# The residual rows behind the first attention: no longer stored by the second projection stage, made again by the last stage

## The chip, the cores and the metric

The kernel is one program on one core of one Trainium2 chip (trn2). TensorE (PE in the profile) does the matmuls, VectorE is DVE, ScalarE is ACT, GpSimd is POOL, and SyncE (SP) only issues transfers. The metric is the device time of one execution in microseconds, lower is better. All data are float32.

## The reference, cut to what matters

Four sub-layers stand one behind the other; each ends with `x = x + layernorm(sublayer(layernorm(x)))` over 4 x 2048 rows of 256 features. The change touches the end of the third and the fourth:

```python
x = x + _layernorm(_L1_attn_ref(_layernorm(x), wq, wk, wv))     # third: attention with 16 heads
x = x + _layernorm(_L1_ffn_ref(_layernorm(x), ...))             # fourth: attention in 4 slices

# inside _L1_ffn_ref, of each slice e of 512 tokens, m = 256 / 2**e
out = einsum('bnm,om->bno', attn_out[:, sl, :m], o_w[:m, :m]) + o_b[:m]   # padded with zeros to 256
outs.append(out + x[:, sl, :])
```

With a = the first attention's output, and x2 the rows ahead of it, the rows behind it are x3 = x2 + a * rstd(a) - mean(a) * rstd(a), where rstd is one over the root of variance plus 1e-5, per row. They are needed twice: in the projections of the fourth sub-layer, and in its last step.

## The kernel before

Rows are worked on in 16 groups of 512 (four of the batch's slices e = 0 to 3, for each of four batch entries b). A group is a tile of 128 partitions by 4 rows (J) by 256 features, 512 KB. The program is a row of stages (`phase_...`), with a barrier of all engines between two of them; each has one in-order instruction list per engine, written out by hand, with semaphores between the lists. Nothing reorders them.

**phase_sliced** (L1354) runs behind the first attention. SP loads a group of `ao1` into A and of `x2` into X, three buffers each (L1415, L1418). DVE takes statistics of A; POOL makes rstd (RS0, L1467 and L1469); DVE adds, X = A * RS0 + X (L1586), and makes NB0 = -mean * RS0 (L1590). The rows in X still lack the shift NB0; the statistics and projections that follow don't need it, since a layernorm takes it out. ACT's `shifted` (L1543) adds it with four Identity instructions of 128x256 into XS (L1544), and SP's `store` (L1423) writes XS to `x3`. Beside it the group goes through a second layernorm (DVE L1596 to L1608), is turned by PE (L1506), copied by ACT (L1551), projected by PE (L1522, L1528), and split into high and low parts (ACT L1560, DVE L1618), which SP stores (L1434, L1438). ACT's list is, for each g: shifted, copy_turned, high. SP's: load(g + 2), store(g), store_qkv(g - 1).

**phase_attention** is the second attention and lies between the two stages that change.

**phase_final** (L2233) loads the attention's output (AT) and `x3` (X, four buffers, L2278), projects AT on PE (L2313), and for each group g: DVE's `add` biases the product (L2353) and makes Z = X * scale + product in the columns below m (L2359); ACT's `rest` makes Z in the other columns (L2326; nothing for e = 0); DVE's `stats` (L2368, L2372); POOL makes the reciprocal root RS with two small instructions (L2298, L2301); DVE's `result` makes NB (L2379) and Z = Z * RS + X (L2383, signals y_done); ACT adds NB into XO (L2339) and issues the store (L2342). The lists:

```python
# DVE:  add(0) stats(0); each g: add(g + 1), stats(g + 1), result(g)
# ACT:  rest(1);         each g: rest(g + 2), XO(g) once y_done(g), wait for XO(g), issue its store
# POOL:                  each g: VE(g), RS(g) once the statistics of g are there
# SP:   load_x(g + 1) waits for result(g - 3), then load_a(g + 1)
```

Of the kernel before, what the change touches and what calls it, by code (L numbers as in the profile page):

```python
# [5 lines left out]
F32 = mybir.dt.float32  # L6
F32R = mybir.dt.float32r
ALU = mybir.AluOpType
# [3 lines left out]
P = 128  # L12
B, T, D = 4, 2048, 256
TOK = B * T
# [1338 lines left out]

def phase_sliced(nc, ao_d, x_d, xnew_d, scales, ident_d, w_d, bias_d, nw_d, nb_d, qk_d, v_d):  # L1354

# [5 lines left out]
    with ExitStack() as ctx:  # L1361
        m = Mem(nc, ctx, tag)
        A = [m.sb(f"A{u}", [P, J, D]) for u in range(NX)]
        X = [m.sb(f"X{u}", [P, J, D]) for u in range(NX)]
        XS, XI = ([m.sb(f"{q}{u}", [P, J, D]) for u in range(2)] for q in ("XS", "XI"))
        XT = [m.sb(f"XT{u}", [P, CC, GT]) for u in range(2)]
        ST0, ST1 = (m.sb(q, [P, J, 6]) for q in ("ST0", "ST1"))
        MV0, MV1 = (m.sb(q, [P, J, 2]) for q in ("MV0", "MV1"))
        VE0, RS0 = (m.sb(q, [P, J]) for q in ("VE0", "RS0"))
        VE1 = m.sb("VE1", [P, 2, J])  # L1370
        NB0 = [m.sb(f"NB0{u}", [P, J]) for u in range(2)]
        nhalf = m.sb("nhalf", [P, 2, J])
# [15 lines left out]
            "const_ld", "half_set", "stat0", "stat1", "var0", "var1", "eps0", "eps1", "rs0", "rs1"))  # L1388
        nb0_done, x_sum, xs_done, xi_done, turned, xt, proj, vproj = (m.sem(n) for n in (
            "nb0_done", "x_sum", "xs_done", "xi_done", "turned", "xt", "proj", "vproj"))  # L1390
        hi_done, lo_done, v_done, nb_wide, w_scaled, b_put, b_done = (m.sem(n) for n in (
            "hi_done", "lo_done", "v_done", "nb_wide", "w_scaled", "b_put", "b_done"))
        a_ld, x_ld = ([m.sem(f"{n}{u}") for u in range(NX)] for n in ("a_ld", "x_ld"))
        xs_st, l_st = ([m.sem(f"{n}{u}") for u in range(2)] for n in ("xs_st", "l_st"))
        block = ctx.enter_context(nc.Block())
# [14 lines left out]
        def _(sp):  # L1410
            def load(g):
                b, e = divmod(g, E4)
                u = g % NX
                wait(sp, x_sum, g - NX + 1)
                sp.dma_start(A[u][:, :, :], ao_d[b][:, e * J:(e + 1) * J, :]).then_inc(a_ld[u], 16)  # L1415
                wait(sp, xi_done, g - NX + 1)
                wait(sp, xs_done, g - NX + 1)
                sp.dma_start(X[u][:, :, :], group(held(x_d), g)).then_inc(x_ld[u], 16)  # L1418

            def store(g):  # L1420
                u = g % 2
                wait(sp, xs_done, g + 1)
                sp.dma_start(group(held(xnew_d), g), XS[u][:, :, :]).then_inc(xs_st[u], 16)  # L1423

# [24 lines left out]
            for g in range(NGR):  # L1449
                if g + 2 < NGR:  # L1450
                    load(g + 2)
                store(g)
                if g > 0:
                    store_qkv(g - 1)
            store_qkv(NGR - 1)
            for u in range(2):
                sp.wait_ge(xs_st[u], 8 * NGR)
                sp.wait_ge(l_st[u], 40 * NGR)

        @block.gpsimd  # L1460
        def _(pool):
            nc.gpsimd.memset(nhalf[:, :, :], -0.5).then_inc(half_set, 1)
            pool.wait_ge(half_set, 1)

            def scale0(g):
                wait(pool, var0, g + 1)
                nc.gpsimd.tensor_scalar(VE0[:, :], MV0[:, :, 1], EPS, None, ALU.add).then_inc(eps0, 1)  # L1467
                wait(pool, eps0, g + 1)
                nc.gpsimd.tensor_tensor(RS0[:, :], VE0[:, :], nhalf[:, 0, :], ALU.pow).then_inc(rs0, 1)  # L1469

            def scale1(g):
                wait(pool, var1, g + 1)
                nc.gpsimd.tensor_scalar(VE1[:, 0, :], MV1[:, :, 1], 1.0 + EPS, EPS * EPS, ALU.mult,
                                        ALU.add).then_inc(eps1, 1)
                nc.gpsimd.tensor_scalar(VE1[:, 1, :], MV1[:, :, 1], EPS, None, ALU.add).then_inc(eps1, 1)
                wait(pool, eps1, 2 * g + 2)
                nc.gpsimd.tensor_tensor(scales[:, g, :, :], VE1[:, :, :], nhalf[:, :, :], ALU.pow).then_inc(rs1, 1)

            scale0(0)
            for g in range(NGR):  # L1480
                scale1(g)
                if g + 1 < NGR:
                    scale0(g + 1)
# [53 lines left out]
        def _(act):  # L1537
            def shifted(g):
                u = g % 2
                wait(act, x_sum, g + 1)  # L1540
                wait(act, nb0_done, g + 1)
                wait(act, xs_st[u], 16 * (g // 2))
                for j in range(J):  # L1543
                    ins = nc.scalar.activation(XS[u][:, j, :], X[g % NX][:, j, :], ACT.Identity,  # L1544
                                               bias=NB0[u][:, j:j + 1])
                ins.then_inc(xs_done, 1)

            def copy_turned(g):
# [15 lines left out]
            for g in range(NGR):  # L1564
                shifted(g)
                copy_turned(g)
                high(g)

        @block.vector
        def _(dve):  # L1570
# [10 lines left out]
            def add(g):  # L1581
                u = g % NX
                wait(dve, rs0, g + 1)
                wait(dve, x_ld[u], 16 * (g // NX + 1))
                for j in range(J):
                    ins = nc.vector.scalar_tensor_tensor(out=X[u][:, j, :], in0=A[u][:, j, :], scalar=RS0[:, j:j + 1],  # L1586
                                                         in1=X[u][:, j, :], op0=ALU.mult, op1=ALU.add)
                ins.then_inc(x_sum, 1)
                wait(dve, xs_done, g - 1)
                nc.vector.scalar_tensor_tensor(out=NB0[g % 2][:, :], in0=MV0[:, :, 0], scalar=-1.0, in1=RS0[:, :],  # L1590
                                               op0=ALU.mult, op1=ALU.mult).then_inc(nb0_done, 1)

# [639 lines left out]

def phase_final(nc, ao_d, ow_d, ob_d, scales, x_d, out_d):  # L2233

# [4 lines left out]
    with ExitStack() as ctx:  # L2239
        m = Mem(nc, ctx, tag)  # L2240
        AT = [m.sb(f"AT{u}", [P, CC, GT]) for u in range(3)]
        X = [m.sb(f"X{u}", [P, J, D]) for u in range(NX)]
        Z = [m.sb(f"Z{u}", [P, J, D]) for u in range(NZ)]
        XO = [m.sb(f"XO{u}", [P, J, D]) for u in range(2)]
# [10 lines left out]
                               "eps", "rs", "y_done", "nb_done", "xo_done"))  # L2255
        x_ld = [m.sem(f"x_ld{u}") for u in range(NX)]
        a_ld = [m.sem(f"a_ld{u}") for u in range(3)]
        o_st = [m.sem(f"o_st{u}") for u in range(2)]
# [7 lines left out]
        def _(sp):  # L2266
# [8 lines left out]

            def load_x(g):
                wait(sp, y_done, g - NX + 1)
                sp.dma_start(X[g % NX][:, :, :], group(held(x_d), g)).then_inc(x_ld[g % NX], 16)  # L2278
# [13 lines left out]
        @block.gpsimd  # L2292
        def _(pool):
            nc.gpsimd.memset(nhalf[:, :], -0.5).then_inc(half_set, 1)
            pool.wait_ge(half_set, 1)
            for g in range(NGR):
                wait(pool, var, g + 1)
                nc.gpsimd.tensor_scalar(VE[g % 2][:, :], MV[g % 2][:, :, 1], EPS, None, ALU.add).then_inc(eps, 1)  # L2298
                wait(pool, eps, g + 1)
                wait(pool, nb_done, g - 1)  # L2300
                nc.gpsimd.tensor_tensor(RS[g % 2][:, :], VE[g % 2][:, :], nhalf[:, :], ALU.pow).then_inc(rs, 1)  # L2301
# [16 lines left out]
        def _(act):  # L2318
            def rest(g):
                e, u = g % E4, g % 2  # L2320
                if e == 0:
                    return
                wait(act, x_ld[g % NX], 16 * (g // NX + 1))
                wait(act, xo_done, g - NZ + 1)
# [3 lines left out]
                ins.then_inc(rest_done, 1)  # L2328

            rest(1)  # L2330
            for g in range(NGR):
                u = g % 2
                if g + 2 < NGR:
                    rest(g + 2)
                wait(act, y_done, g + 1)
# [11 lines left out]
        def _(dve):  # L2347
            def add(g):
# [6 lines left out]
                wait(dve, biased, g + 1)  # L2355
                wait(dve, x_ld[g % NX], 16 * (g // NX + 1))
                wait(dve, xo_done, g - NZ + 1)
# [38 lines left out]
def sandwich(nc, d, out_d):  # L2396
# [4 lines left out]
    ycat = dram("ycat", [2 * CC, P, TOK])  # L2401
    x1, xn2, x2, x3 = (dram(n, [TOK, D]) for n in ("x1", "xn2", "x2", "x3"))
    logits, routed = (dram(n, [B, EXPERTS, T]) for n in ("logits", "routed"))
# [8 lines left out]

    with nc.sbuf_tensor("scales", [P, NG, 2, J], F32) as scales:
        phase_norm_x(nc, tokens(d["x"]), ident, xnT)
# [4 lines left out]
        phase_attention(nc, "at1", HEADS1, DH1, DH1 ** -0.5, qk1, v1, ao1, ident)  # L2419
        phase_sliced(nc, ao1, x2, x3, scales, ident, d["wqkv2"], d["bias2"], d["norm_w"], d["norm_b"], qk2, v2)  # L2420
        phase_attention(nc, "at2", HEADS2, DH2, D ** -0.5, qk2, v2, ao2, ident, units=sliced_units())
        phase_final(nc, ao2, d["o_w"], d["o_b"], scales, x3, out_d)

# [56 lines left out]
```

## Time and profile before

| what | value |
|---|---|
| median of 3 runs | 5150.57 us (5149.77 to 5151.31) |
| span of the profiled execution, which is its own time here | 5142.3 us |
| median less that span | 8.3 us |
| busy in the span | PE 92%, DVE 82%, ACT 67%, POOL 26% |
| phase_sliced | from 3936.3 us (its first transfer is issued) to 4155.3 us (the first of the next stage) |
| phase_final | from 5035.9 us to the end |

The profile is of one execution; times of rows are us from the span's start. Busy shares are over the whole span and say little of the two stages that change, so the rows below are of stretches inside those.

### The profile page before, as it was taken

The page shows a single profiled execution, that of the slowest core. Times are in us where ns is not written, and L with a number is a line of the kernel's source. Part 1 is how long each engine was busy: PE and PEld are TensorE (multiplying, and loading weights), DVE is VectorE, ACT ScalarE, POOL GpSimd, SP SyncE. Part 2 cuts the span into 40 slices and gives each one's busy share as a digit, 9 for nine tenths or more (in the row PEclk, how much of TensorE's full clock was granted, in tenths as well). Part 3 has the DMA queues.
Part 4 walks back from the last instruction along what each step waited for, and adds up shares of the span by engine and source line. Part 5 has one row for each costly group of instructions (what it writes and reads, how often), then busy time and mean ns, then how long its engine had stood idle before and what let it go on. Part 6 is the DMA issues. An engine that isn't in the chain of part 4 may idle for free. (4 is left out here: it accounts for less than half of the span.)

```text
span 5142.3 us, 90411 instructions
## 1 busy us (share of the span) xinstructions
PE 4714.6 (92%) x34043; PEld 2092.5 (41%) x34043; DVE 4237.0 (82%) x5517; ACT 3449.7 (67%) x6176; POOL 1333.4 (26%) x881
## 2 busy tenths in 40 slices
PE   6999786797999999999999999999998879999993
PEld 3444452364333333333333333333334445555542
DVE  6999650397899999999999999999993877777736
ACT  4787310132688888888888888888886326666663
POOL 2233220164000000000000000000001229999992
PEclk9999897898899999999999999999998669999996
DMA  5110479688333333343333344333322941222305
GB/s 182 52 53 33 155 247 385 251 280 232 45 53 48 48 48 48 54 54 51 48 48 48 50 54 53 50 48 48 49 34 76 313 128 42 71 70 67 78 10 167
DMA packets 390773, 498.42 MB, mean 97 GB/s; under 512 B 165440, under 2 KB 278880, under 8 KB 373312
## 3 DMA queue, kind: packets, MB, share of 16 engines
q1 hardware_dynamic: 372448, 465.90, 38.7%
q10 hardware_dynamic: 17888, 26.74, 1.5%
q8 instruction: 268, 4.39, 0.4%
q14 instruction: 169, 1.38, 0.1%
HBM read 325.15 MB, written 165.02 MB: 95 GB/s over the span
## 5 line engine op out<-in xcount | busy, mean ns | idle before, releaser
L792 DVE TENSOR_REDUCE at_NM<-at_MX 128x1 f32<-128x1024 f32 (+1 forms) x3008 | 3085.0, 1050 | 299.5 <-PE at_MX L614 270.9
L734 ACT ACTIVATE at_PB<-at_S 128x512 f32<-128x512 f32 x5056 | 2719.4, 597 | 585.9 <-PE at_S L643 466.0
L614 PE MATMUL at_MX<-at_KT,at_QT 48*128 48x512 f32 (+1 forms) x5056 | 1919.7, 455 | 60.2 <-DMA at_VS<-v 45.6
L643 PE MATMUL at_S<-at_QT,at_KT 50*128 50x512 f32 (+1 forms) x5056 | 1899.9, 441 | 6.0 <-ACT at_PB L734 5.8
L655 PE MATMUL at_AV<-at_PB,at_VS 128*32 128x256 f32 (+1 forms) x18304 | 1567.7, 414 | 16.7 <-ACT at_AVS L742 15.7
L643 PEld LDWEIGHTS at_S<-at_QT,at_KT 50*128 50x128 f32 (+1 forms) x5056 | 801.8, 187 | 876.6 <-ACT at_PB L734 772.0
L614 PEld LDWEIGHTS at_MX<-at_KT,at_QT 48*128 48x128 f32 (+1 forms) x5056 | 791.6, 190 | 311.0 <-DVE at_NM L792 217.7
L655 PEld LDWEIGHTS at_AV<-at_PB,at_VS 128*32 128x32 f32 x18304 | 364.6, 108 | 858.6 <-ACT at_PB L734 745.4
L548 POOL CAST at_NMR<-at_NMF 16x128 fp32r<-16x128 f32 x79 | 22.1, 280 | 1625.3 <-ACT at_NMF L747 1625.3
L575 POOL TENSOR_TENSOR at_SUM<-at_SUM,at_PB 128x2048 f32<-128x2048 f32 x90 | 415.4, 4615 | 10.9
L932 PE MATMUL wkv_PQ<-wkv_XT,wkv_WT 128*128 128x512 f32 x768 | 339.6, 600 | 42.5 <-DVE wkv_DL L1052 25.9
L575 POOL TENSOR_TENSOR at_SUM<-at_PB 128x2048 f32<-128x2048 f32 x75 | 352.0, 4697 | 29.9 <-ACT at_PB L734 29.7
L558 POOL TENSOR_TENSOR at_O<-at_FO,at_REC 128x256 f32<-128x256 f32 x64 | 39.8, 622 | 1008.2 <-DVE at_REC L803 1008.2
L932 PEld LDWEIGHTS wkv_PQ<-wkv_XT,wkv_WT 128*128 128x128 f32 x768 | 144.6, 191 | 237.1 <-issue 192.6
L1011 POOL TENSOR_TENSOR wkv_EV<-wkv_E2S,wkv_V 128x1024 f32<-128x1024 f32 x32 | 75.6, 2361 | 355.3 <-DVE wkv_MN L1030 153.3
L945 PE MATMUL wkv_NP<-wkv_T,wkv_ident 128*128 128x512 f32 x256 | 120.7, 616 | 15.8 <-DVE wkv_T L1067 15.8
L1234 PE MATMUL r_PA<-r_OC,r_A 128*128 128x256 f32 x512 | 114.7, 384 | 12.5 <-DMA r_A<-ycat 12.5
L1836 PE MATMUL r_QK<-r_WC,r_XT 128*128 128x512 f32 x256 | 122.0, 601 | 0.5 <-DVE r_WC L1995 0.5
L1234 PEld LDWEIGHTS r_PA<-r_OC,r_A 128*128 128x128 f32 x512 | 97.6, 193 | 26.0 <-DVE r_OC L1343 13.3
L1522 PE MATMUL r_PO<-r_XT,r_WS 128*128 128x512 f32 (+2 forms) x136 | 91.4, 833 | 17.8 <-ACT r_XT L1551 17.8
L991 ACT ACTIVATE wkv_PD<-wkv_PD 128x1024 f32<-128x1024 f32 x32 | 33.8, 1057 | 107.2 <-DVE wkv_PD L1084 107.2
L2165 ACT ACTIVATE moe_HS<-moe_PH 128x1024 f32<-128x1024 f32 x8 | 8.2, 1023 | 144.0 <-PE moe_TP L2210 120.5
(209 smaller groups left out, 3531.4 us busy)
## 6 DMA issues: line engine op xcount, KB each, us to landing
moe_W<-in_w SPq DMA_DIRECT2D x64, 1024.0 KB, 11.9
at_QT<-qk SPq DMA_DIRECT2D x402, 128.0 KB, 5.2
at_KT<-qk SPq DMA_DIRECT2D x384, 128.0 KB, 6.6
qk<-r_HI SPq DMA_DIRECT2D x52, 512.0 KB, 5.0
qk<-r_LO SPq DMA_DIRECT2D x52, 512.0 KB, 5.3
at_VS<-v SPq DMA_DIRECT2D x96, 256.0 KB, 9.2
at_KT<-qk SPq DMA_DIRECT2D x96, 256.0 KB, 6.2
ycat<-wkv_Y SPq DMA_DIRECT2D x32, 512.0 KB, 2.6
```

The costliest lines, as they stand in the source:

```text
L575: nc.gpsimd.tensor_tensor(total[:, :, :], other, PB[:, k:k + NCH, :], ALU.add).then_inc(sum_done, 1)
L614: ins = nc.tensor.matmul(MX[r][:, a, :], q_of(s)[h:h + NQ, b * P:(b + 1) * P], k_of(it, s, b * P // W)[h:h + NQ, (c + a) * W:(c + a + 1) * W],
L643: nc.tensor.matmul(SP_[item(it, s, "score", t)[1]][:, :], k_of(it, s, c)[h:h + NQ + 2, kb * P:(kb + 1) * P], q_of(s)[h:h + NQ + 2, c * W:( ...
L655: ins = nc.tensor.matmul(AV[c * VW:(c + 1) * VW, cols], v_of(it, s, c)[:, kb, :], PB[:, (NCH * kb + c) % NPB, cols], start=first, stop=last)
L734: nc.scalar.activation(PB[:, t % NPB, :], SP_[r][:, :], ACT.Exp, scale=scale).then_inc(exp_done, 1)
L792: nc.vector.tensor_reduce(NM4[:, b, c:c + 1], MX[r][:, :, :].rearrange("p a n -> p (a n)"), AX_X, ALU.max, negate=True).then_inc(ring_got, 1)
L932: ins = nc.tensor.matmul(PQ[q][:, tt * 512:(tt + 1) * 512], WT[:, cc, row:row + P], XT[b % 2][:, cc, t0:t0 + 512], start=(cc == 0), stop=( ...
L945: ins = nc.tensor.matmul(NP[:, t], ident[:, :], part[s][:, t], start=(k == 0), stop=(k == 1))
L1011: nc.gpsimd.tensor_tensor(EV[s][:, :], E2S[s][:, :], V[s][:, :], ALU.mult).then_inc(pv, 1)
L1234: ins = nc.tensor.matmul(PA[u][:, j, :], A[u][:, q, j * P:(j + 1) * P], OC[:, q, :], start=(q == 0), stop=(q == NC - 1))
L1522: ins = nc.tensor.matmul(PO[a][:, h, :], WS[0:k, c, lo:lo + P], XT[u][0:k, c, :], start=(c == 0), stop=(c == len(ks) - 1))
L1836: ins = nc.tensor.matmul(QK[j % 2][:, :], XT[u][:, c, j * P:(j + 1) * P], WC[:, c, 0:2 * D], start=(c == 0), stop=(c == CC - 1))
```

## The change

`phase_sliced` no longer makes XS and no longer stores `x3`; the tensor is gone. Instead it leaves rstd and -mean * rstd of each group in an SBUF tensor `outer` (128 x 16 x 2 x 4), which lives through to the last stage, as `scales` already did. `phase_final` loads two tiles for each group, A from `ao1` and X from `x2`; ACT's new `shift` makes A * rstd + NB0 in place (four instructions of 128x256), and POOL's new `add_rows` adds it to X (one instruction of 128x1024). All readers of X now wait for x_sum in place of the load.

```diff
 phase_sliced:
-        XS, XI = ([m.sb(f"{q}{u}", [P, J, D]) for u in range(2)] for q in ("XS", "XI"))
+        XI = [m.sb(f"XI{u}", [P, J, D]) for u in range(2)]
-                wait(sp, xs_done, g - NX + 1)
-            def store(g):
-                u = g % 2
-                wait(sp, xs_done, g + 1)
-                sp.dma_start(group(held(xnew_d), g), XS[u][:, :, :]).then_inc(xs_st[u], 16)
-                store(g)
+            sp.wait_ge(nb0_done, NGR)
-                sp.wait_ge(xs_st[u], 8 * NGR)
-                nc.gpsimd.tensor_tensor(RS0[:, :], VE0[:, :], nhalf[:, 0, :], ALU.pow).then_inc(rs0, 1)
+                nc.gpsimd.tensor_tensor(outer[:, g, 0, :], VE0[:, :], nhalf[:, 0, :], ALU.pow).then_inc(rs0, 1)
-            def shifted(g):
-                ...
-                for j in range(J):
-                    ins = nc.scalar.activation(XS[u][:, j, :], X[g % NX][:, j, :], ACT.Identity,
-                                               bias=NB0[u][:, j:j + 1])
-                ins.then_inc(xs_done, 1)
-                shifted(g)
-                wait(dve, xs_done, g - 1)
-                nc.vector.scalar_tensor_tensor(out=NB0[g % 2][:, :], in0=MV0[:, :, 0], scalar=-1.0, in1=RS0[:, :],
+                nc.vector.scalar_tensor_tensor(out=outer[:, g, 1, :], in0=MV0[:, :, 0], scalar=-1.0,
+                                               in1=outer[:, g, 0, :], op0=ALU.mult, op1=ALU.mult).then_inc(nb0_done, 1)
 phase_final:
+        A = [m.sb(f"A{u}", [P, J, D]) for u in range(NX)]
             def load_x(g):
+                b, e = divmod(g, E4)
+                wait(sp, x_sum, g - NX + 1)
+                sp.dma_start(A[g % NX][:, :, :], first_d[b][:, e * J:(e + 1) * J, :]).then_inc(x_ld[g % NX], 16)
                 wait(sp, y_done, g - NX + 1)
                 sp.dma_start(X[g % NX][:, :, :], group(held(x_d), g)).then_inc(x_ld[g % NX], 16)
 pool:
+            def add_rows(g):
+                wait(pool, x_ld[g % NX], 32 * (g // NX + 1))
+                wait(pool, shifted, g + 1)
+                nc.gpsimd.tensor_tensor(X[g % NX][:, :, :], X[g % NX][:, :, :], A[g % NX][:, :, :],
+                                        ALU.add).then_inc(x_sum, 1)
+            add_rows(0)
+            add_rows(1)
             for g in range(NGR):
+                if g + 2 < NGR:
+                    add_rows(g + 2)
                 wait(pool, var, g + 1)
                 ...
 act, rest(g):
-                wait(act, x_ld[g % NX], 16 * (g // NX + 1))
+                wait(act, x_sum, g + 1)
 act:
+            def shift(g):
+                wait(act, x_ld[g % NX], 32 * (g // NX + 1))
+                for j in range(J):
+                    ins = nc.scalar.activation(A[g % NX][:, j, :], A[g % NX][:, j, :], ACT.Identity,
+                                               bias=outer[:, g, 1, j:j + 1], scale=outer[:, g, 0, j:j + 1])
+                ins.then_inc(shifted, 1)
+            shift(0)
+            shift(1)
             rest(1)
             for g in range(NGR):
                 u = g % 2
                 if g + 2 < NGR:
+                    shift(g + 2)
                     rest(g + 2)
                 wait(act, y_done, g + 1)
                 ...
 dve, add(g):
-                wait(dve, x_ld[g % NX], 16 * (g // NX + 1))
+                wait(dve, x_sum, g + 1)
```

## Rows read from the trace of the kernel before

**Rows 1.** Busy time by stretch: us, busy (instructions) of each engine, PE clock, DMA share, GB/s
```profile
4040.00:4080.00 40.00, 34.18 (x96) 20.00 (x94) 32.09 (x93) 15.71 (x29) 10.50 (x16) 0.71 0.90 298
...
5036.00:5046.00 10.00, 5.39 (x18) 4.56 (x19) 0.00 (x0) 0.00 (x0) 0.00 (x0) 0.60 0.89 287
...
5080.00:5100.00 20.00, 7.68 (x35) 6.45 (x34) 18.41 (x64) 10.39 (x26) 5.05 (x7) 0.67 0.70 234
```

**Rows 2.** Waits, 3936 to 4145 us: who for whom, us in total, times, longest
```profile
ACT r_XT L1551 <- PE r_PT L1506: 44.0, 16, 11.3
...
PE r_PO L1522 <- ACT r_XT L1551: 17.8, 16, 1.1
...
DVE r_ST L1574 <- DMA r_A<-ao: 9.7, 1, 9.7
```

**Rows 3.** Groups of instructions in that stretch: busy, mean ns, idle before
```profile
L1544 ACT ACTIVATE r_XS<-r_X,r_NB 128x256 f32<-128x256 f32 x64 | 27.1, 501 | 17.9 <-DVE r_NB L1590 17.9
```

**Rows 4.** Waits of SP's queue, 3936 to 4150 us
```profile
SPq L1423 <- ACT r_XS L1544: 73.1, 13, 19.8
```

**Rows 5.** Transfers, 3936 to 4145 us: totals; one issue line with median us to landing
```profile
DMA packets 36519, 57.59 MB, mean 276 GB/s; under 512 B 3080, under 2 KB 18652, under 8 KB 36508
...
x<-r_XS SPq DMA_DIRECT2D x16, 512.0 KB, 5.5
```

**Rows 6.** Instructions in order of time at the end of that stage: start, us
```profile
4136.98 0.33 SPq L1423 DMA_DIRECT2D x<-r_XS  x1
...
4150.68 0.36 SPq L1438 DMA_DIRECT2D v<-r_VB  x1
```

**Rows 7.** Waits, 5034 us to the end
```profile
POOL fin_VE L2298 <- DVE fin_NB L2379: 55.3, 14, 8.1
...
ACT fin_XO L2339 <- DVE fin_Z L2383: 41.9, 16, 6.8
DVE fin_PA L2353 <- PE fin_PA L2313: 20.9, 4, 14.3
```

**Rows 8.** In order of time, start of the last stage
```profile
5046.08 1.28 ACT L2326 ACTIVATE fin_Z<-fin_X,scales 128x128 f32<-128x128 f32 x4 [14.96 <-DMA fin_X<-x]
...
5050.50 0.38 DVE L2372 BATCH_NORM_AGGREGATE fin_MV<-fin_ST 128x2 f32<-128x6 f32 x4
...
5051.05 0.23 POOL L2298 TENSOR_SCALAR fin_VE<-fin_MV 128x4 f32<-128x4 f32 x1 [15.05 <-DVE fin_MV L2372]
5051.36 1.04 POOL L2301 TENSOR_TENSOR fin_RS<-fin_VE,fin_nhalf 128x4 f32<-128x4 f32 x1
...
5054.44 1.66 DVE L2383 SCALAR_TENSOR_TENSOR fin_Z<-fin_Z,fin_RS,fin_X 128x256 f32<-128x256 f32 x4
```

**Rows 9.** In order of time, inside the last stage
```profile
5078.60 1.66 DVE L2383 SCALAR_TENSOR_TENSOR fin_Z<-fin_Z,fin_RS,fin_X 128x256 f32<-128x256 f32 x4
...
5080.30 1.70 ACT L2339 ACTIVATE fin_XO<-fin_Z,fin_NB 128x256 f32<-128x256 f32 x4 [1.54 <-DVE fin_Z L2383]
...
5082.52 1.60 ACT L2326 ACTIVATE fin_Z<-fin_X,scales 128x224 f32<-128x224 f32 x4 [0.51 <-ACT fin_XO L2339]
...
5083.44 0.44 POOL L2298 TENSOR_SCALAR fin_VE<-fin_MV 128x4 f32<-128x4 f32 x1 [3.08 <-DVE fin_NB L2379]
5083.97 1.12 POOL L2301 TENSOR_TENSOR fin_RS<-fin_VE,fin_nhalf 128x4 f32<-128x4 f32 x1
```

**Rows 10.** In order of time, end of the last stage
```profile
5128.27 1.67 DVE L2383 SCALAR_TENSOR_TENSOR fin_Z<-fin_Z,fin_RS,fin_X 128x256 f32<-128x256 f32 x4
...
5133.36 1.12 POOL L2301 TENSOR_TENSOR fin_RS<-fin_VE,fin_nhalf 128x4 f32<-128x4 f32 x1
...
5134.60 1.67 DVE L2383 SCALAR_TENSOR_TENSOR fin_Z<-fin_Z,fin_RS,fin_X 128x256 f32<-128x256 f32 x4
```

**Rows 11.** One line's instructions (an early stage): ns min/median/max, first and last start
```profile
L1011 POOL TENSOR_TENSOR wkv_EV<-wkv_E2S,wkv_V x32: 2351/2362/2370, 93.1 to 553.9; 128x1024 f32<-128x1024 f32 x32
```

**Rows 12.** Transfers, 5035 to 5142 us: totals
```profile
DMA packets 13350, 21.16 MB, mean 198 GB/s; under 512 B 800, under 2 KB 9376, under 8 KB 13344
```

More of the change, by code:

```diff
@@ L1351, in _, with phase_sliced @@
                     stats_a(g + 1)
-def phase_sliced(nc, ao_d, x_d, xnew_d, scales, ident_d, w_d, bias_d, nw_d, nb_d, qk_d, v_d):
+def phase_sliced(nc, ao_d, x_d, outer, scales, ident_d, w_d, bias_d, nw_d, nb_d, qk_d, v_d):
     E4 = T // GT
@@ L1368, in phase_sliced @@
         MV0, MV1 = (m.sb(q, [P, J, 2]) for q in ("MV0", "MV1"))
-        VE0, RS0 = (m.sb(q, [P, J]) for q in ("VE0", "RS0"))
+        VE0 = m.sb("VE0", [P, J])
         VE1 = m.sb("VE1", [P, 2, J])
-        NB0 = [m.sb(f"NB0{u}", [P, J]) for u in range(2)]
         nhalf = m.sb("nhalf", [P, 2, J])
@@ L1388, in phase_sliced @@
             "const_ld", "half_set", "stat0", "stat1", "var0", "var1", "eps0", "eps1", "rs0", "rs1"))
-        nb0_done, x_sum, xs_done, xi_done, turned, xt, proj, vproj = (m.sem(n) for n in (
-            "nb0_done", "x_sum", "xs_done", "xi_done", "turned", "xt", "proj", "vproj"))
+        nb0_done, x_sum, xi_done, turned, xt, proj, vproj = (m.sem(n) for n in (
+            "nb0_done", "x_sum", "xi_done", "turned", "xt", "proj", "vproj"))
         hi_done, lo_done, v_done, nb_wide, w_scaled, b_put, b_done = (m.sem(n) for n in (
@@ L1393, in phase_sliced @@
         a_ld, x_ld = ([m.sem(f"{n}{u}") for u in range(NX)] for n in ("a_ld", "x_ld"))
-        xs_st, l_st = ([m.sem(f"{n}{u}") for u in range(2)] for n in ("xs_st", "l_st"))
+        l_st = [m.sem(f"l_st{u}") for u in range(2)]
         block = ctx.enter_context(nc.Block())
@@ L1537, in _ @@
         def _(act):
-            def shifted(g):
[L1539 to L1542, printed above, removed]
-                for j in range(J):
-                    ins = nc.scalar.activation(XS[u][:, j, :], X[g % NX][:, j, :], ACT.Identity,
-                                               bias=NB0[u][:, j:j + 1])
-                ins.then_inc(xs_done, 1)
             def copy_turned(g):
@@ L1585, in add @@
                 for j in range(J):
-                    ins = nc.vector.scalar_tensor_tensor(out=X[u][:, j, :], in0=A[u][:, j, :], scalar=RS0[:, j:j + 1],
+                    ins = nc.vector.scalar_tensor_tensor(out=X[u][:, j, :], in0=A[u][:, j, :], scalar=outer[:, g, 0, j:j + 1],
                                                          in1=X[u][:, j, :], op0=ALU.mult, op1=ALU.add)
                 ins.then_inc(x_sum, 1)
-                wait(dve, xs_done, g - 1)
-                nc.vector.scalar_tensor_tensor(out=NB0[g % 2][:, :], in0=MV0[:, :, 0], scalar=-1.0, in1=RS0[:, :],
-                                               op0=ALU.mult, op1=ALU.mult).then_inc(nb0_done, 1)
+                nc.vector.scalar_tensor_tensor(out=outer[:, g, 1, :], in0=MV0[:, :, 0], scalar=-1.0,
+                                               in1=outer[:, g, 0, :], op0=ALU.mult, op1=ALU.mult).then_inc(nb0_done, 1)
             def stats_x(g):
@@ L2230, in _, with phase_final @@
                 out(g)
-def phase_final(nc, ao_d, ow_d, ob_d, scales, x_d, out_d):
+def phase_final(nc, ao_d, ow_d, ob_d, outer, scales, first_d, x_d, out_d):
     E4 = T // GT
@@ L2256, in phase_final @@
         x_ld = [m.sem(f"x_ld{u}") for u in range(NX)]
+        shifted, x_sum = m.sem("shifted"), m.sem("x_sum")
         a_ld = [m.sem(f"a_ld{u}") for u in range(3)]
@@ L2401, in sandwich @@
     ycat = dram("ycat", [2 * CC, P, TOK])
-    x1, xn2, x2, x3 = (dram(n, [TOK, D]) for n in ("x1", "xn2", "x2", "x3"))
+    x1, xn2, x2 = (dram(n, [TOK, D]) for n in ("x1", "xn2", "x2"))
     logits, routed = (dram(n, [B, EXPERTS, T]) for n in ("logits", "routed"))
@@ L2411, in sandwich @@
     ident = d["ident"]
-    with nc.sbuf_tensor("scales", [P, NG, 2, J], F32) as scales:
+    with nc.sbuf_tensor("outer", [P, NG, 2, J], F32) as outer, nc.sbuf_tensor("scales", [P, NG, 2, J], F32) as scales:
         phase_norm_x(nc, tokens(d["x"]), ident, xnT)
@@ L2419, in sandwich @@
         phase_attention(nc, "at1", HEADS1, DH1, DH1 ** -0.5, qk1, v1, ao1, ident)
-        phase_sliced(nc, ao1, x2, x3, scales, ident, d["wqkv2"], d["bias2"], d["norm_w"], d["norm_b"], qk2, v2)
+        phase_sliced(nc, ao1, x2, outer, scales, ident, d["wqkv2"], d["bias2"], d["norm_w"], d["norm_b"], qk2, v2)
         phase_attention(nc, "at2", HEADS2, DH2, D ** -0.5, qk2, v2, ao2, ident, units=sliced_units())
-        phase_final(nc, ao2, d["o_w"], d["o_b"], scales, x3, out_d)
+        phase_final(nc, ao2, d["o_w"], d["o_b"], outer, scales, ao1, x2, out_d)
 def kernel(**inputs):
```

## The prediction

> **What bounds the kernel now.** The busy shares of the whole span don't help, so I read by stage: first busy time by stretch, then the waits of the two stages that change, then instructions in order of time where a wait looked close.
>
> In the stage behind the first attention PE is busy 34.2 of 40 us and DVE 32.1, ACT only 15.7, while the transfer engines are busy at 0.90 and move 298 GB/s [rows 1]. The reader should see three things in its waits [rows 2]. ACT's copy of the turned tile waits for PE in all 16 groups, 44.0 us in sum, so whatever ACT does ahead of it (the four XS instructions among it) is over before PE is. PE in turn waits for that copy 1.1 us in each group. And DVE waits for a load once, for the very first. This stage is a loop of PE, ACT's copy and PE, with DVE close behind; ACT has slack, and the transfers, busy as they are, hold up nobody.
>
> In the last stage DVE is busy 18.4 of 20 us [rows 1]. ACT waits for DVE's result in every group, and POOL waits for DVE's statistics (14 and 2 times); DVE's one large wait is for PE, 4 times, 14.3 of its 20.9 us at the start [rows 7]. So DVE sets the pace: 13 groups from the first result's end, 5054.44 + 1.66 = 5056.10 [rows 8], to result 13's, 5128.27 + 1.67 = 5129.94 [rows 10], which is 73.84 / 13 = 5.68 us for a group.
>
> **Part 1, taken out of the earlier stage.** 64 ACT instructions, 27.1 us busy [rows 3]. Nobody waits for them but SP, and the copy behind them waits for PE [rows 2]: 0 us. 16 stores of 512 KB go, 8.39 MB of the 57.59 [rows 5]. SP stood 73.1 us at the head of its line for XS [rows 4]; without that wait it gets earlier to the query and key stores, but the only readers of those buffers' freedom are ACT and DVE two groups later, and neither shows a wait for it [rows 2]. At the end the last XS store was issued 13.7 us before the last value store [rows 6], with a landing time of 5.5 us [rows 5], so the stage's end doesn't hang on it. 0 us. The bounds: below, if the transfers were the stage's limit, 8.39 MB / 276 GB/s = 30.4 us gained; above, nothing is added, since RS0 and NB0 only change their place. I take 0, nearest to the single wait for a load, and keep 3 us of gain for the range.
>
> **Part 2, put into the last stage: a new loop.** What decides is the order in three lists. ACT, in its turn g, does shift(g + 2) only behind XO(g - 1), and XO(g - 1) waits for result(g - 1). POOL, in its turn g, does add_rows(g + 2) before VE(g) and RS(g), and add_rows(g + 2) waits for shift(g + 2). DVE's result(g) waits for RS(g). So result(g) now follows result(g - 1) through ACT and POOL, though the rows that are summed there are needed only two groups later. Before, VE(g) and RS(g) had to wait for the statistics alone. One turn of this loop:
>
> - RS ready to result finished: RS ended at 5133.36 + 1.12 = 5134.48, the result at 5134.60 + 1.67 = 5136.27 [rows 10]: 1.79 us
> - to XO's start, 5080.30 less 5078.60 + 1.66 = 5080.26 [rows 9]: 0.03
> - XO, four instructions [rows 9]: 1.70
> - wait for XO, issue of its store, next instruction: 0.51, the idle time ahead of `rest` [rows 9]
> - shift, four of 128x256 with a scale and a bias, not in the trace. XO, same size with a bias alone, takes 1.70 and XS's single ones 501 ns [rows 3]; unoverlapped it were 4 x 0.50 = 2.00, and 128x224 with a scale is 1.60 [rows 9]. I take 1.70, bounds 1.60 and 2.00
> - ACT to POOL: 0.05. Nearest, DVE to XO, 0.03; upper bound 0.17: POOL's VE started at 5051.05 behind DVE's statistics, which ended at 5050.88 [rows 8]
> - add_rows: 2.36, the same shape as L1011 [rows 11], bounds below
> - to VE: 0.06, as between VE's end 5051.28 and RS at 5051.36 [rows 8]
> - VE and RS: 5051.05 to 5052.40 = 1.35 [rows 8], or 5083.44 to 5085.09 = 1.65 beside a running result (VE was let go by DVE's NB, right ahead of one) [rows 9]
>
> Sum: 1.79 + 0.03 + 1.70 + 0.51 + 1.70 + 0.05 + 2.36 + 0.06 + 1.35 = 9.55 us, against 5.68. What else a group needs runs beside this: DVE's add and stats of the next group, 4.0 us on average (5.68 less a result of 1.67), start behind result(g - 1) and are over well before RS(g), which comes 9.55 - 1.79 = 7.76 us behind it; ACT's rest(g + 2), up to 1.60, starts at add_rows' end, and XO(g) doesn't come before 1.35 + 1.79 = 3.14 us later. POOL's own work, 3.8 us, and ACT's, 5.5, are each far below 9.55; it is the row of them that costs.
>
> VE takes 0.23 us with no result running [rows 8] and 0.44 beside one, whose both inputs lie in SBUF [rows 9]. In the new loop the result is over 3.9 us before add_rows starts, and the next waits for RS, so I take 1.35 and 2.36 as they stand. The Trainium skill, "SBUF — State Buffer", section "Who interferes with whom", says that a DVE instruction with two SBUF inputs blocks a GpSimd instruction that reads SBUF for its whole length, and that one with a single SBUF input doesn't; the two VE rows agree in direction. By that rule nothing on DVE could stretch add_rows here; if instead the statistics beside it slowed POOL as a result does, VE's ratio would be applied to add_rows, and the sum would be that of the second rival.
>
> **Start and end of the last stage.** The second X tile (256 + 512 + 128 + 512 + 256 + 512 = 2176 KB into the queue, the rest being weights, bias and AT) was there at 5046.08 [rows 8]. Now two more tiles are ahead of that point: 1.05 MB more at 287 GB/s [rows 1] is 3.7 us, so shift(1) starts at 5049.7, ends 5051.4; add_rows(1) to 5053.8; rest(1), 1.28 us, to 5055.1; the third pair, 3.7 us later than the second, is in by 5053.4, so shift(2) runs to 5056.8 and add_rows(2) to 5059.3; VE and RS to 5060.7; result(0) to 5062.5, against 5056.10. Then 13 turns, since add_rows(3) to add_rows(15) stand before RS(1) to RS(13): 5062.5 + 13 x 9.55 = 5186.6, against 5129.94: +56.7 us. From there to the end nothing is added: 5142.3 - 5129.94 = 12.4 us as before.
>
> Transfers: a group moves 21.16 / 16 = 1.32 MB [rows 12], and now 0.52 MB more, 1.85 MB. At 298 GB/s [rows 1] that is 6.2 us, below 9.55: hidden. Under a turn of 5.68 us it would not be.
>
> **The sum.** 5142.3 + 56.7 = 5199.0 for the profiled execution; the median of the runs lies 8.3 us above its span, so 5207 us.
>
> **The rivals.** The likeliest case (chance 0.82) is the loop above. Its own range goes by the bounds: 0.10 us less for shift in one turn, or 0.30 + 0.12 + 0.30 more for shift, the step to POOL and VE/RS: 13 turns make -1 to +9 us, the start +-4 (about one tile pair's 3.7), part 1 down to -3: 5199 to 5220.
>
> Second (0.08): POOL's sum is stretched by DVE beside it. VE's ratio 0.44 / 0.23 applied to the part of add_rows beside DVE's statistics, at most 2.36 x 0.91 = 2.1 us in a turn, 13 turns: up to +28, so about 5220 to 5235. Against it: L1011's 32 instances spread by only 19 ns [rows 11] and DVE's 4.0 us behind a result are about over when add_rows begins, 3.99 us behind it.
>
> Third (0.06): ACT's and POOL's new work lies beside DVE's after all, and DVE keeps the pace at 5.68 us. Only the later start stays, 6.4 us: 5157. For it speaks that ACT has 9.6 of 20 us free and POOL 15.0 [rows 1], and each engine's sum fits; against it, that POOL's RS(g) can't pass add_rows(g + 2) in its list.
>
> Fourth, the other side (0.04): the transfers bound the earlier stage (0.90 busy [rows 1]), and the stores' absence gives back up to 30.4 us. It turns the sign only if the last stage costs less than that, so if its turn stays under 5.68 + (30.4 - 6.4) / 13 = 7.5 us; with the pace of the third rival the time is 5150.6 + 6.4 - 30.4 = 5127. With the loop at 9.55 it would still be 5207 - 30 = 5177, slower than before. Against it: one wait for a load in the whole stage [rows 2].
>
> **How the numbers follow.** Forecast 5207. The range is the first case's own with 4 to 5 us at each side for gaps between engines that no row shows, and a part of the second: 5195 to 5225, some 0.83 of the chance. A measurement of this kernel tells about 0.2% (10 us) from no change, so faster is below 5140, slower above 5161. First and second are slower, 0.90; the third is the same, 0.06; of the fourth 0.03 is faster, and 0.01 slower, where only its first half holds. Faster 0.03, same 0.06, slower 0.91.
>
> **What would show it.** In the profile after: DVE waits for POOL's RS (at NB, L2379's successor) about 14 times, 3 to 4.5 us each, where it didn't before; POOL's add_rows waits for ACT's shift; the starts of XO lie 9.5 us apart from group 1 to 13, alike for all four e, since nothing of the loop depends on e; add_rows takes 2.36 us and shift 1.70 for four; the last stage is some 57 us longer, and the earlier one within 3 us of its length. I am wrong if XO's distance is under 8 us or over 10.5, if POOL's RS(g) ends before add_rows(g + 2), or if the earlier stage gets shorter by more than 3 us.

## The result and the profile after

The changed kernel takes 5209.17 us (median of 4 runs, 5207.17 to 5215.17), the kernel before in the same set 5150.94: a ratio of 1.0117, 95% interval 1.0102 to 1.0131, 58 us slower. The forecast was 5207.

The instructions of the loop follow one another in time as the prediction has them. These rows are one full turn of the changed kernel's last stage (start, us, engine, line), from one result to the next:

```profile
5072.75 1.71 ACT L2345 ACTIVATE fin_XO<-fin_Z,fin_NB 128x256 f32<-128x256 f32 x4 [1.61 <-DVE fin_Z L2389]
...
5074.97 2.07 ACT L2329 ACTIVATE fin_A<-fin_A,outer 128x256 f32<-128x256 f32 x4 [0.51 <-ACT fin_XO L2345]
5075.42 0.38 DVE L2378 BATCH_NORM_AGGREGATE fin_MV<-fin_ST 128x2 f32<-128x6 f32 x4
5077.18 2.34 POOL L2285 TENSOR_TENSOR fin_X<-fin_X,fin_A 128x1024 f32<-128x1024 f32 x1 [6.25 <-ACT fin_A L2329]
...
5079.49 0.23 POOL L2294 TENSOR_SCALAR fin_VE<-fin_MV 128x4 f32<-128x4 f32 x1
...
5079.80 1.03 POOL L2297 TENSOR_TENSOR fin_RS<-fin_VE,fin_nhalf 128x4 f32<-128x4 f32 x1
5080.86 0.16 DVE L2385 SCALAR_TENSOR_TENSOR fin_NB<-fin_MV,fin_RS 128x4 f32<-128x4 f32 x1 [5.07 <-POOL fin_RS L2297]
5080.94 1.67 DVE L2389 SCALAR_TENSOR_TENSOR fin_Z<-fin_Z,fin_RS,fin_X 128x256 f32<-128x256 f32 x4
```

The reader should see that XO, shift, sum, VE, RS and result stand end to end, although three engines do them. Beside them lie only DVE's add and statistics of the next group (beside XO and shift) and ACT's rest (beside VE and RS). DVE, whose statistics ended at 5075.80, does nothing for 5.07 us. In the kernel before, DVE went straight on: in all 16 groups together it stood idle for 0.1 us in front of NB, the first instruction of a result (busy us, mean ns, idle before):

```profile
L2379 DVE SCALAR_TENSOR_TENSOR fin_NB<-fin_MV,fin_RS 128x4 f32<-128x4 f32 x16 | 2.1, 131 | 0.1
```

The same in the waits of the changed kernel, from 5034 us to the end (who for whom, us in total, times, longest):

```profile
POOL fin_X L2285 <- ACT fin_A L2329: 96.7, 16, 11.1
...
DVE fin_NB L2385 <- POOL fin_RS L2297: 63.5, 14, 5.3
ACT fin_XO L2345 <- DVE fin_Z L2389: 38.0, 16, 5.6
ACT fin_Z L2322 <- POOL fin_X L2285: 30.2, 12, 2.5
...
DVE fin_PA L2359 <- PE fin_PA L2309: 14.1, 1, 14.1
```

DVE's wait for RS is new; its wait for PE, 4 times before [rows 7], is left only at the start, since PE now has time. POOL's wait for the statistics has become one for shift. ([rows 7] put the old wait down to NB, and the prediction says so too for one VE; in the code VE waits for the statistics alone, and NB follows these at once.)

Busy time between the end of result 0 and the end of result 13, to about 3 us, first the kernel before, then the changed one (us, then busy of PE, PE's loads, DVE, ACT, POOL, the clock, the transfers' share, GB/s):

```profile
5056.00:5130.00 74.00, 29.56 (x120) 25.11 (x120) 66.00 (x236) 36.87 (x93) 20.44 (x27) 0.64 0.65 218
```

```profile
5075.00:5200.00 125.00, 34.87 (x120) 28.76 (x120) 64.08 (x226) 62.08 (x140) 47.32 (x41) 0.55 0.55 172
```

DVE did the same 64 to 66 us of work in 125 us in place of 74. No engine is busy for more than 0.52 of the time, and the transfers are busy at 0.55, at 172 GB/s in place of 218. With no engine and no queue near its full time, the stage is bound by a chain from one to the next.

**Where the 58 us are.** In the traces each stage can be told by its first transfer. The last stage lasts 5213.2 - 5046.4 = 166.8 us, before 142.3 - 35.9 = 106.4: +60.4. The stage behind the first attention, 3943.7 to 4164.9, lasts 221.2 us against 219.0, the second attention 881.5 against 880.6. This execution was the longest of the four (5215.17 us) and entered the changed part 7.4 us later than the one before, although nothing ahead of it differs; a kernel below with the same program up to there entered it at 3935.7. So the 70.9 us between the two spans are 60.4 of the change and 10.5 of executions differing, and the last stage's own length is the measure that I use for small terms from here on.

### The profile page after: what moved, and what is told of

The parts are those of the page before. It is cut to its first block and busy times, and to the rows that moved or that the text cites. A ratio compares the mean times of both kernels' runs of the same rounds, so it can differ in the third digit from the quotient of the medians.

```text
span 5213.2 us, 90413 instructions
## 1 busy us (share of the span) xinstructions
PE 4733.7 (91%) x34043; PEld 2095.1 (40%) x34043; DVE 4239.4 (81%) x5517; ACT 3458.7 (66%) x6176; POOL 1364.7 (26%) x897
## 5 line engine op out<-in xcount | busy, mean ns | idle before, releaser
L614 PE MATMUL at_MX<-at_KT,at_QT 48*128 48x512 f32 (+1 forms) x5056 | 1924.4, 456 | 58.2 <-DMA at_VS<-v 43.5
L614 PEld LDWEIGHTS at_MX<-at_KT,at_QT 48*128 48x128 f32 (+1 forms) x5056 | 792.9, 190 | 310.6 <-DVE at_NM L792 221.2
L2309 PE MATMUL fin_PA<-fin_OW,fin_AT 128*128 128x256 f32 (+3 forms) x160 | 45.1, 453 | 101.3 <-DMA fin_AT<-ao 101.3
```

Source lines behind the costliest of these rows:

```text
L614: ins = nc.tensor.matmul(MX[r][:, a, :], q_of(s)[h:h + NQ, b * P:(b + 1) * P], k_of(it, s, b * P // W)[h:h + NQ, (c + a) * W:(c + a + 1) * W],
```

## The experiments

Last-stage lengths below are the span less the start of the first load of that stage, each from one profile. e2, e4 and e6 leave out a part of the arithmetic, so they serve for timing alone. The kernel before ran beside each set, its median between 5148.87 and 5150.94; the ratios are to the runs of the same set.

| kernel | median us | ratio to before (95%) | last stage us |
|---|---|---|---|
| before | 5150.94 | | 106.4 |
| changed | 5209.17 | 1.0117 (1.0102 to 1.0131) | 166.8 |
| e2_first_part | 5148.70 | 0.9998 (0.9986 to 1.0010) | 107.0 |
| e3_last_part | 5211.11 | 1.0121 (1.0103 to 1.0139) | 167.2 |
| e4_bias_only | 5205.31 | 1.0113 (1.0100 to 1.0126) | 161.8 |
| e6_quarter_sum | 5185.71 | 1.0073 (1.0060 to 1.0086) | 142.7 |
| e1_pool_order | 5176.39 | 1.0054 (1.0039 to 1.0069) | 132.4 |
| e9_shift_ahead | 5169.94 | 1.0043 (1.0025 to 1.0061) | 124.8 |
| e5_ahead | 5157.56 | 1.0017 (1.0005 to 1.0030) | 111.8 |
| e7_ahead_at | 5145.35 | 0.9996 (0.9986 to 1.0006) | 102.9 |
| e8_before_at | 5142.51 | 0.9988 (0.9980 to 0.9997) | 99.9 |

**The two halves of the change, alone.**

```diff
 e2_first_part, against the kernel before
-                wait(sp, xs_done, g - NX + 1)
-                store(g)
-                shifted(g)
-                wait(dve, xs_done, g - 1)
-        phase_final(nc, ao2, d["o_w"], d["o_b"], scales, x3, out_d)
+        phase_final(nc, ao2, d["o_w"], d["o_b"], scales, x2, out_d)
```

> The kernel before, with the XS rows of the earlier stage neither made nor stored, and its last stage loading x2 in their place, so that its output lacks the first attention's part in the last sum. It is the first half of the change alone. Theory 1 (nobody waited for XS or its store): the stage between the attentions keeps its 219 us within 2, the time is 5151 within 3. Rival (transfers bound that stage, 0.90 busy): 8.39 MB less at 276 GB/s, up to 30 us less, 5121 to 5140.

Measured: 5148.70 us, ratio 0.9998; the stage took 4156.9 - 3937.9 = 219.0 us, as before within 0.2.

```diff
 e3_last_part, against the changed kernel
+                    ins = nc.scalar.activation(XS[u][:, j, :], X[g % NX][:, j, :], ACT.Identity,
+                                               bias=outer[:, g, 1, j:j + 1])
+                sp.dma_start(group(held(xnew_d), g), XS[u][:, :, :]).then_inc(xs_st[u], 16)
+                store(g)
+                shifted(g)
```

> The changed kernel, but the earlier stage still makes XS and stores it as before (nobody reads it). It is the second half of the change alone. Theory 1: equal to the changed kernel, 5209 within 4, last stage 166 to 167 us long. Rival (the stores' absence gave back something that hid a larger loss): above 5215.

Measured: 5211.11 us, last stage 167.2 us. The two halves add up, 0 and 60: 27 us of ACT's work and 8.39 MB of stores were worth nothing where they stood, in a stage whose transfers were busy at 0.9. The rival of a stage bound by transfers has fallen.

**The size of two terms of the loop.**

```diff
 e4_bias_only, against the changed kernel
-                                               bias=outer[:, g, 1, j:j + 1], scale=outer[:, g, 0, j:j + 1])
+                                               bias=outer[:, g, 1, j:j + 1])
 e6_quarter_sum, against the changed kernel
-                nc.gpsimd.tensor_tensor(X[g % NX][:, :, :], X[g % NX][:, :, :], A[g % NX][:, :, :],
+                nc.gpsimd.tensor_tensor(X[g % NX][:, 0, :], X[g % NX][:, 0, :], A[g % NX][:, 0, :],
```

> The changed kernel with shift's scale left out (a bias alone), so the rows of A are not multiplied by their rstd. It sizes one term. In the changed kernel the four shift instructions take 2.07 us and single ones 588 ns, where XO's four take 1.70. If the second per-partition operand makes that difference, single ones fall to about 496 ns, the four to 1.70, and the loop's turn from 9.87 to 9.50: 13 x 0.37 = 4.8 us less, 5204. If it is the place (in place, from a freshly loaded tile), shift keeps 2.07 us and the time 5209.

> The changed kernel with POOL adding one of the four row blocks of each group, the other three left without the first attention's part. It sizes POOL's term. Theory 1 (the sum stands whole in the loop): the instruction falls from 2.34 to about 0.62 us (a 128x256 sum on POOL elsewhere in this kernel takes 0.62), the turn from 9.87 to 8.15, 13 x 1.72 = 22 us less and 1 to 2 at the start: about 5185. Theory 2 (the loads or ACT's shift hold the pace, the sum lies beside them): 5205 to 5210.

These rows group instructions (busy, mean ns); the changed kernel's shift, then that of e4_bias_only:

```profile
L2329 ACT ACTIVATE fin_A<-fin_A,outer 128x256 f32<-128x256 f32 x64 | 33.2, 588 | 21.6 <-DMA fin_X<-x 15.6 <-ACT fin_XO L2345 6.0
```

```profile
L2329 ACT ACTIVATE fin_A<-fin_A,outer 128x256 f32<-128x256 f32 x64 | 27.3, 498 | 22.4 <-DMA fin_X<-x 16.4 <-ACT fin_XO L2345 6.0
```

The second operand per partition costs 90 ns an instruction, and the last stage is 5.0 us shorter without it (4.8 expected). The sum, in the changed kernel and in e6_quarter_sum:

```profile
L2285 POOL TENSOR_TENSOR fin_X<-fin_X,fin_A 128x1024 f32<-128x1024 f32 x16 | 37.5, 2342 | 96.7 <-ACT fin_A L2329 96.7
```

```profile
L2285 POOL TENSOR_TENSOR fin_X<-fin_X,fin_A 128x256 f32<-128x256 f32 x16 | 11.6, 723 | 98.5 <-ACT fin_A L2329 98.5
```

1.62 us less, 13 times, is 21.0; two more sums, those of groups 1 and 2, stand in the chain ahead of result(0), which ends 3.2 us sooner (23.1 us into the stage against 26.3). Together 24.2, and the stage is 24.1 us shorter. A microsecond taken from either instruction comes back whole: both stand in the loop.

**Undoing the dependency with all the work kept.** Three kernels keep all the work and change the order of the lists; two of them also give A's loads a semaphore of their own, so that shift can go ahead of X's load.

```diff
 e1_pool_order, against the changed kernel
             for g in range(NGR):
-                if g + 2 < NGR:
-                    add_rows(g + 2)
                 wait(pool, var, g + 1)
                 ...
                 nc.gpsimd.tensor_tensor(RS[g % 2][:, :], VE[g % 2][:, :], nhalf[:, :], ALU.pow).then_inc(rs, 1)
+                if g + 2 < NGR:
+                    add_rows(g + 2)
 e5_ahead, against e1_pool_order
-                wait(act, x_ld[g % NX], 32 * (g // NX + 1))
+                wait(act, f_ld[g % NX], 16 * (g // NX + 1))     # A has a load semaphore of its own
             shift(1)
+            shift(2)
-                if g + 2 < NGR:
-                    shift(g + 2)
-                    rest(g + 2)
+                if g + 3 < NGR:
+                    shift(g + 3)
+                if g + 2 < NGR:
+                    rest(g + 2)
 e9_shift_ahead: e5_ahead with POOL's list as in the changed kernel
```

> The changed kernel with one thing moved: POOL makes VE(g) and RS(g) ahead of add_rows(g + 2), not behind it. Theory 1 (the loss is the loop result, XO, shift, add_rows, RS, result): RS(g) comes free of the loop, DVE's wait at NB for RS falls from 63.5 us to under 15. But ACT's rest(g + 2) still waits for add_rows(g + 2) in front of XO(g), so ACT's own list sets the turn where e of g + 2 isn't 0: XO 1.70 + 0.51 + shift 2.07 + 0.05 + sum 2.34 + 0.03 + rest 1.45 = 8.15 us, and about 5.7 in the fourth: 7.5 on average against 9.87. 13 x 2.4 = 31 us less: about 5178. Theory 2 (POOL's sum, or the doubled loads, slow DVE or the transfers by being there at all, whatever the order): the same work is done, so 5205 to 5212.

> The changed kernel with both lists cut loose: POOL makes RS(g) ahead of add_rows(g + 2), ACT shifts group g + 3 (loaded under a semaphore of its own) ahead of rest(g + 2), so that no shift, sum and rest of one group follow each other within a turn. The work is the same. Theory 1: ACT's turn is 1.70 + 0.51 + 2.07 + 1.1 on average = 5.4 us, POOL's 3.8, DVE's 5.68 sets the pace again; only the start stays later by about 6 us: 5157, DVE's wait at NB for RS under 5 us. Theory 2 (the added work costs by being there: port, transfers): above 5185.

> The other half of e5_ahead alone: ACT shifts group g + 3 a turn early (with A's own load semaphore), while POOL keeps the changed kernel's order, add_rows(g + 2) ahead of VE(g) and RS(g). Theory 1 (the loss is the dependency from result(g - 1) through XO and shift to the sum, not the place of the sum in POOL's list): shift(g + 2) ends 0.03 + 1.70 + 0.51 + 2.07 = 4.3 us behind result(g - 2), the sum follows (unless X's load, issued at that same point, lands later than 4.3 us; it takes 4 to 7), so RS(g) is ready some 8.1 to 10.8 us behind result(g - 2), where result(g) needs it at 2 x 5.68 - 1.8 = 9.6. DVE's pace or little more: 5155 to 5165. Rival (POOL's order costs by itself, RS behind a sum of 2.34 us): as e1_pool_order was worth 33 us, the order must be undone too, and this one stays above 5175.

e1_pool_order gave 5176.39 us, where about 5178 was expected: the order of POOL's list alone is 34 of the 60 us. Its waits in the last stage show what came next:

```profile
ACT fin_Z L2322 <- POOL fin_X L2285: 31.2, 12, 2.8
```

ACT stands 31 us in front of rest(g + 2) for the sum that it has just fed itself, which holds XO(g) behind it. DVE no longer waits for RS at all. The theory did not have a second cost that its trace shows: four of the 16 results take 3.75 us in place of 1.67, which makes 8.3 us (26.7 busy in the changed kernel). e9_shift_ahead below shows from what.

```profile
L2389 DVE SCALAR_TENSOR_TENSOR fin_Z<-fin_Z,fin_RS,fin_X 128x256 f32<-128x256 f32 x64 | 35.0, 608 | 0.0
```

e5_ahead gave 5157.56 us. With the same instructions, the same loads and the same 37.6 us of sums on POOL, 55 of the 60 us are gone (last stage 111.8 us). So the work costs at most 5 us by being there; the rest of the loss was its place in three in-order lists.

e9_shift_ahead missed both of its expectations: 5169.94, neither 5155 to 5165 nor over 5175. The dependency is gone, DVE waits for RS 1.7 us in all, but something else stretches DVE. Its group of results against that of e5_ahead, first e9_shift_ahead, then e5_ahead:

```profile
L2392 DVE SCALAR_TENSOR_TENSOR fin_Z<-fin_Z,fin_RS,fin_X 128x256 f32<-128x256 f32 x64 | 39.2, 675 | 0.0
```

```profile
L2392 DVE SCALAR_TENSOR_TENSOR fin_Z<-fin_Z,fin_RS,fin_X 128x256 f32<-128x256 f32 x64 | 26.7, 478 | 0.0
```

12.5 us more in the same 64 instructions; NB takes 1.9 more (4.0 against 2.1), and DVE's idle time is 1.7 less. That is 12.7 of the 13.0 us by which its last stage is longer (124.8 against 111.8). In order of time in e9_shift_ahead:

```profile
5078.24 3.75 DVE L2392 SCALAR_TENSOR_TENSOR fin_Z<-fin_Z,fin_RS,fin_X 128x256 f32<-128x256 f32 x4
...
5078.58 2.34 POOL L2286 TENSOR_TENSOR fin_X<-fin_X,fin_A 128x1024 f32<-128x1024 f32 x1 [2.03 <-ACT fin_A L2330]
```

Four instructions that take 1.67 us alone take 3.75, 2.08 more, when POOL's sum starts among them; this happens in six of the 16 groups. Both read two SBUF operands. The Trainium skill, "SBUF — State Buffer", section "Who interferes with whom", calls the contention for the ports that VectorE shares with GpSimd an exclusive lock, names a VectorE instruction with two SBUF inputs as one that contends with a GpSimd instruction that reads SBUF, and says that issue order decides who blocks. The 2.08 us, little less than the sum's 2.34, agree with a wait of nearly a whole sum; no run here tells the port from another cause of the same length. In the changed kernel the loop itself keeps the two apart (result 478 to 480 ns, sum 2342 ns), and in e5_ahead POOL's sum falls behind the result (478 ns): so the order of POOL's list is worth 13 us beside the dependency. RS first is not enough by itself, as the four long results of e1_pool_order show; what counts is whether a sum starts during a result.

**What was left, and a version 0.1% faster than the kernel before.** In e5_ahead DVE still waited for PE at the full-width groups, as it does before [rows 7], since the attention's output is loaded behind a load that waits for a result.

```diff
 e7_ahead_at, against e5_ahead; e8_before_at, the same against the kernel before
+            load_a(2)
             for g in range(2, NGR):
-                load_a(g)
                 if g + 1 < NGR:
+                    load_a(g + 1)
                     load_x(g + 1)
```

> e5_ahead with SP issuing the attention output's load of group g + 1 ahead of the loads of A and X of group g + 1, where the latter wait for result(g - 3). In e5_ahead DVE waits 3 times about 2.6 us for PE at a full-width group, whose 512 KB came late. If DVE's pace is what is left, that wait goes: up to 7.8 us less than e5_ahead, about 5150, the time of the kernel before. If the three loads and a store of each group are now limited by the transfers, nothing is gained: 5155 to 5158.

> The kernel before with the same one change of SP's order. DVE waits there 3 times 2.2 us for PE behind a late load [20.9 - 14.3 us]. If DVE sets the pace, 6 us less: 5144. It is also the yardstick for e7_ahead_at: if both are freed of that wait, e7 should stand 3 to 6 us above this one, by its later start.

e8_before_at: 5142.51 us, ratio 0.9988 (0.9980 to 0.9997), last stage 99.9 us, 6.5 shorter. DVE's wait for PE in e8_before_at:

```profile
DVE fin_PA L2354 <- PE fin_PA L2314: 14.7, 1, 14.7
```

One time in place of 4 [rows 7], and about 6 us, as expected. e7_ahead_at: 5145.35 us, where about 5150 was expected, and its last stage is 8.9 us shorter than that of e5_ahead. It is not to be told from the kernel before (0.9986 to 1.0006) in the total; its last stage is 3.5 us shorter than there and 3.0 us longer than that of e8_before_at. The expectation put such a difference down to a later start. In the traces the start is only 0.5 us of it (result(0) ends 21.1 us into the stage against 20.7); the other 2.4 are in the loop, whose results lie 5.33 us apart on average against 5.15, and there DVE waits for ACT's rest:

```profile
DVE fin_ST L2378 <- ACT fin_Z L2324: 2.3, 4, 1.2
```

The best kernel of the study is thus the kernel before with its loads reordered; the change itself, freed of the waits named here, is still 3 us behind that one and gives nothing.

## Why the prediction was right

- **Part 1, worth nothing:** confirmed by e2_first_part and e3_last_part, from both sides. What told it was one list of waits: no wait for a load but the first, none for a store, and ACT's copy waiting for PE in all groups.
- **The loop:** confirmed. The distances of the 13 results lie between 9.83 and 9.90 us, alike for all four e. The mean distance of the results, (5200.78 - 5072.71) / 13, is 9.85 us against the 9.55 forecast. By term: RS to result's end 1.78 (1.79), to XO 0.04 (0.03), XO 1.71 (1.70), to shift 0.51 (0.51), shift 2.07 (1.70), to POOL 0.14 (0.05), sum 2.34 (2.36), to VE nothing (0.06), VE and RS 1.34 (1.35). The step to POOL and the missing step to VE cancel, each by 0.09. The one large miss is shift: I took XO's 1.70, which has one operand per partition, for an instruction with two. 0.37 x 13 = 4.8 us. Even the upper bound, 2.00, was too low, since it multiplied a one-operand duration. The page "ScalarE: Activation LUTs" of the Trainium skill, in its section "What ACT_TABLE_LOAD costs", puts each per-partition pointer operand at about 93 ns; the runs agree with 90 (588 against 498). An estimate by that page's figure would have been 1.70 + 4 x 0.093 = 2.07. With the longer turn DVE's wait for RS went up to 5.3 us, 4.5 on average, where 3 to 4.5 were forecast.
- **The start:** result(0) ended 26.3 us into the stage against 20.2 before, 6.1 later (6.4 forecast). Here two errors cancel, by luck: shift(1) could start 12.9 us into the stage where 13.8 was reckoned, and the two shifts in this chain each took 0.37 longer. The end is 12.4 us long in both, as forecast.
- **The sum of it:** 6.1 + 13 x (9.85 - 5.68) = 60.3 us, the 60.4 of the stages' lengths; forecast 56.7, so 3.7 short. The medians differ by 58.2, which holds both within its interval (53 to 67 us); that the median came out only 2 us above the forecast is luck, within what executions differ by.
- **The pace of 5.68 us before** was not DVE's own, though the prediction takes it so: 6.6 of DVE's 20.9 us of waiting for PE lie inside those groups, and without them e8_before_at runs at 5.15. The sum doesn't suffer, since 5.68 was measured and the new loop hides that wait too.
- **The transfers:** hidden under the turn, as forecast. The remark that a group's 1.85 MB need 6.2 us and would show under a turn of 5.68 was wrong: e7_ahead_at moves 1.85 MB a group at a turn of 5.33, with DVE waiting for PE only at the start. The 298 GB/s of [rows 1] was what one stage moved, not a limit; between results 0 and 13 of e7_ahead_at it is 307. There ACT does wait for loads of A, 6.9 us in all after the first, so a part of DVE's 2.3 us for ACT's rest may be theirs.
- **VE and the sum unstretched:** right, and for the reason given: no result runs beside them. The second rival, a sum stretched beside DVE, didn't occur here (its 16 instances span 2338 to 2352 ns), nor did the statistics slow it anywhere. In e1_pool_order and e9_shift_ahead a sum was stretched beside results, to 2.65 us at most, with the larger loss on DVE's side, which the rival did not have.
- **The third rival,** DVE keeping the pace at 5157, was wrong for this program and came close for e5_ahead (5157.56): its mechanism, DVE keeping the pace, is what the change would be with its lists in another order. That the number agrees to the microsecond is luck: the ten runs of e5_ahead span 5144.9 to 5167.6, and its last stage is 5.4 us longer than before, of which the later start is 2.8 (result(0) ends 23.0 us into the stage) and not 6.4, and the loop 2.5 (5.87 against 5.68 a turn).

## What to carry to other kernels

When work goes to idle engines, don't add up each engine's free time; follow one datum round the in-order lists and see whether a result of this group now waits, through the new instruction's place in a list, for the result of the group before. The new instruction belongs behind the small ones that the bound engine waits for, and what feeds it a turn earlier. And work that nobody waits for is worth nothing when removed, however busy its queue looks.

## What the runs showed of the hardware

- An Identity activation of 128x256 with scale and bias both per partition takes 588 ns against 498 with a bias alone, also where four overlap (2.07 against 1.70 us).
- A two-input VectorE instruction that meets a GpSimd sum of 128x1024 lasts up to 2.57 us in e1_pool_order (median of the 64 in results 478 ns) and 2.60 in e9_shift_ahead; even the 128x4 NB took up to 1.08 and 1.91 us in place of 0.13. The sum itself took up to 2.65 in place of 2.34. Instructions with one SBUF input kept their durations in kernels with and without the sum: statistics 413 to 414 ns on average, the scaling in add 334 to 335.
- Executions differed by up to 8 us in where this part began (3935.7 to 3943.7), with nothing changed ahead of it; the length of the stage behind the first attention repeated better (219.0 us before, 219.0 in e2_first_part, 219.4 in e3_last_part, 219.1 in e5_ahead), except for 221.2 in the changed kernel, 221.3 in e1_pool_order and 221.8 in e4_bias_only. The other kernels without the copy and the store took 219.0 to 219.4, so removing the copy and the store doesn't cost these 2 us each time; the three kernels that keep them (before, e3_last_part, e8_before_at) never showed it. What it is stays open.
